# A four-layer graph network on one core: weights loaded in two sets, later waits, an early matrix chunk, and another split of the sorting columns

## The reference

```python
h = relu(layernorm(x)); x = x + L0(h)   # h' = h @ Wn.T; sum over edges of [h'[src], |h'[dst]-h'[src]|] @ We.T; mean; linear
h = relu(layernorm(x)); x = x + L1(h)   # 2 transformer layers: q,k,v; per edge softmax over dst; Wo; FFN 128-512-128 with gelu
h = relu(layernorm(x)); x = x + L2(h)   # relu(D_in^-1/2 A (D_out^-1/2 h) @ W + b)
h = relu(layernorm(x)); x = x + L3(h)   # two GCN convolutions (128-128-64), linear, sigmoid
```

## Time and profile before

| | us |
|---|---|
| median of 3 runs | 7202.54 (7202.37 to 7202.93) |
| the profiled execution's own time | 7193.32 |
| its span, first to last instruction | 7191.1 |
| PE / PEld / DVE / ACT / POOL busy in it | 5421.6 / 3619.8 / 4405.4 / 2900.3 / 3153.2 |
| mean granted TensorE clock | 0.905 of full speed |

### The profile page before, as it was taken

The page is one execution under the profiler, slowest core; times in us unless marked ns, Lnnn a source line. Parts: engine busy times, 40 slices in busy tenths (PEclk is TensorE's granted clock), DMA queues, the critical chain, the costliest instruction groups (busy, mean ns, idle before and its releaser), DMA issues. The chain is left out here.

```text
span 7191.1 us, 122531 instructions
## 1 busy us (share of the span) xinstructions
PE 5421.6 (75%) x28121; PEld 3619.8 (50%) x28122; DVE 4405.4 (61%) x12956; ACT 2900.3 (40%) x5577; POOL 3153.2 (44%) x3144
## 2 busy tenths in 40 slices
PE   7967975777777656666666756666666799999998
PEld 3433433666666545555554545555554444444433
DVE  8969967777777477777777368888885311100000
ACT  2532541677776325555555425555553200000000
POOL 3763772777777007666665007777771000000000
PEclk9989986999999768888888869888887899999999
DMA  0000002555556216666666016666663377777799
GB/s 23 0 3 1 0 0 64 170 171 172 172 172 159 56 39 202 198 199 197 199 198 175 4 43 198 196 196 190 192 194 67 130 289 287 273 286 286 291 417 389
DMA packets 466069, 1168.32 MB, mean 162 GB/s; under 512 B 113598, under 2 KB 176638, under 8 KB 433692
## 3 DMA queue, kind: packets, MB, share of 16 engines
q1 hardware_dynamic: 337228, 892.75, 33.5%
q0 software_dynamic: 126464, 273.15, 15.6%
q10 hardware_dynamic: 2256, 0.89, 0.1%
HBM read 759.86 MB, written 405.32 MB: 162 GB/s over the span
## 5 line engine op out<-in xcount | busy, mean ns | idle before, releaser
L698 POOL DMA_INDIRECT ACC<-tab_kv,STAGE x1664 | 1652.2, 993 | 1440.1 <-DMA STAGE<-IDX 744.0
L1219 ACT ACTIVATE PS<-PS,X 128x512 f32<-128x512 f32 x1456 | 968.4, 665 | 534.4 <-PE PS L904 513.8
L892 PE MATMUL PS<-SCR 128*128 128x137 f32 x3328 | 593.8, 329 | 689.9 <-DVE ACC L1717 681.2
L698 POOL DMA_INDIRECT SCR<-tab_h,STAGE x832 | 829.3, 997 | 345.5 <-issue 275.3
L892 PEld LDWEIGHTS PS<-SCR 128*128 128x128 f32 x3328 | 493.6, 219 | 834.8 <-DVE ACC L1717 791.3
L1717 DVE TENSOR_TENSOR ACC<-ACC,PS 128x137 f32 (+1 forms) x2288 | 746.8, 326 | 248.6 <-PE PS L896 133.6
L1060 PE MATMUL PS<-ACC,Q 128*128 128x512 f32 (+3 forms) x2548 | 842.0, 574 | 59.6 <-DMA ACC<-adj 59.6
L659 POOL DMA_INDIRECT placed<-ACC,X x624 | 649.6, 1041 | 422.4 <-DVE X L1488 219.3
L874 PEld LDWEIGHTS PS<-Q,SCR 128*128 128x128 f32 x4992 | 717.3, 213 | 172.7 <-issue 147.3
L874 PE MATMUL PS<-Q,SCR 128*128 x4992 | 758.2, 300 | 57.5 <-issue 50.1
L765 PE MATMUL PS<-Q 128*128 128x416 f16 x3968 | 721.8, 340 | 59.1 <-DVE Q L1511 59.1
(11 more groups left out here) (297 smaller groups left out, 7437.7 us busy)
## 6 DMA issues: line engine op xcount, KB each, us to landing
ACC<-adj SPq DMA_DIRECT2D x252, 1792.0 KB, 6.7
adj<-X SPq DMA_DIRECT2D x936, 256.0 KB
adj<-ITEM SPq DMA_DIRECT2D x520, 256.0 KB
ACC<-tab_kv,STAGE POOLq DMA_INDIRECT x1664
SCR<-tab_h,STAGE POOLq DMA_INDIRECT x832
tab_kv<-SCR SPq DMA_DIRECT2D x14, 896.0 KB, 4.1
placed<-ACC,X POOLq DMA_INDIRECT x624
ACC<-adj SPq DMA_DIRECT2D x21, 448.0 KB, 4.1
```

Source lines behind the costliest of these rows:

```text
L698: nc.gpsimd.indirect_dma_start(G[:, q, j, 0:w], None, table, bass.IndirectOffsetOnAxis(STAGE[:, u, q * S4 + j:q * S4 + j + 1], 0))\
L892: ins = nc.tensor.matmul(dst, oh, M[:, u % 2, j, :], start=True, stop=True)
L1219: nc.scalar.activation(CLASS_SUM[(k + 1) % 2], CLASS_SUM[k % 2], ACT.Copy, scale=KEEP[:, bass.ds(i, 1)])\
```

## The change

PE's share of the sorting columns becomes 504 (o = 1) and 536 (o = 0), POOL's 280 and 296. `load_l1` is split: `load_d` (14 transfers, what phase d needs) with semaphore `w_d`, `load_e` (8 transfers, what phase e needs) with `w_e`. Layer 1's `load_d` is issued by SP inside att0, behind the first two index loads; its `load_e` after phase e of layer 0. Phase d waits for `w_d`, phase e for `w_e`. DVE's wait for x stands right ahead of the instruction that adds it. SP issues the first matrix chunk in phase e of layer 1, once the last aggregate has been read out of the buffer's place.

```diff
-PROD_COLS = [512, 480]
+PROD_COLS = [536, 504]
...
+        D_MATS, D_ROWS, D_COLUMNS = L1MATS[0:4], [n for n in L1ROWS if n not in ("bo", "b2")], L1COLUMNS[0:2]
+        E_MATS, E_ROWS, E_COLUMNS = L1MATS[4:], ["bo", "b2"], L1COLUMNS[2:]
+        D_LOADS, E_LOADS = len(D_MATS + D_ROWS + D_COLUMNS), len(E_MATS + E_ROWS + E_COLUMNS) + 3
...
-            def load_l1(l):
+            def load_d(l):
+                for n in D_MATS:
+                    sp.dma_start(l1mat[n], a[n][l]).then_inc(w_d, 16)
...
+            def load_e(l):
+                for n in E_MATS:
+                    sp.dma_start(l1mat[n], a[n][l]).then_inc(w_e, 16)
...
-            load_l1(0)
+            load_d(0)
+            load_e(0)
...
                 load(0, 0)
                 load(1, 1)
+                if name == "att0":
+                    load_d(1)
...
+            def tiles(k, g, q):
+                m = chunk(k, g, q)
+                sp.dma_start(TILES3[m % 3][:, :, 0:width(g)], adj[g][:, q * QJ:(q + 1) * QJ, 0:width(g)])\
+                    .then_inc(tiles_in[m % 3], 16)
...
                 if l == 1:
                     sp.dma_start(X[:, :, :], x_rows).then_inc(x_back, 16)
+                    wait(sp, dE[1], "ag", NG)
+                    tiles(0, 0, 0)
                 end_phase(sp, "sp")
                 if l == 0:
-                    load_l1(1)
+                    load_e(1)
...
                         if m >= 3:
                             sp.wait_ge(tiles_used, m - 2)
-                        sp.dma_start(TILES3[m % 3][:, :, 0:width(g)], adj[g][:, q * QJ:(q + 1) * QJ, 0:width(g)])\
-                            .then_inc(tiles_in[m % 3], 16)
+                        if m:
+                            tiles(k, g, q)
...
(DVE; PE and ACT alike)
-                dve.wait_ge(w_l1, 16 * L1LOADS * (l + 1))
+                dve.wait_ge(w_d, 16 * D_LOADS * (l + 1))
...
                 s = dE[l]
-                if l == 1:
-                    dve.wait_ge(x_back, 16)
+                dve.wait_ge(w_e, 16 * E_LOADS * (l + 1))
...
                     if l == 1:
+                        dve.wait_ge(x_back, 16)
                         tail.link(V.tensor_tensor(turn_of(X, g), turn_of(X, g), turn_of(Y, g), ALU.add))
```

More of the change, by code:

```diff
@@ L288, in build @@
         LOADS = len(MATS) + len(BIASES) + 3
-        L1LOADS = len(L1MATS) + len(L1ROWS) + len(L1COLUMNS) + 3
+        D_MATS, D_ROWS, D_COLUMNS = L1MATS[0:4], [n for n in L1ROWS if n not in ("bo", "b2")], L1COLUMNS[0:2]
+        E_MATS, E_ROWS, E_COLUMNS = L1MATS[4:], ["bo", "b2"], L1COLUMNS[2:]
+        D_LOADS, E_LOADS = len(D_MATS + D_ROWS + D_COLUMNS), len(E_MATS + E_ROWS + E_COLUMNS) + 3
         def over_tiles(b, n=TG):
@@ L303, in heads @@
             return ap.rearrange("p t (h d) -> p t h d", h=HEADS)
-        edges_in, x_in, w_in, w_l1, x_pad = sem("edges_in"), sem("x_in"), sem("w_in"), sem("w_l1"), sem("x_pad")
+        edges_in, x_in, w_in, x_pad = sem("edges_in"), sem("x_in"), sem("w_in"), sem("x_pad")
+        w_d, w_e = sem("projection_weights_in"), sem("ffn_weights_in")
         const_ready, const_step = sem("const_ready"), sem("const_step")
@@ L481, in _ @@
         def _(sp):
-            def load_l1(l):
-                for n in L1MATS:
-                    sp.dma_start(l1mat[n], a[n][l]).then_inc(w_l1, 16)
-                for n in L1ROWS:
+            def load_d(l):
+                for n in D_MATS:
+                    sp.dma_start(l1mat[n], a[n][l]).then_inc(w_d, 16)
+                for n in D_ROWS:
                     v = a[n][l, 0] if n == "Wdeg" else a[n][l]
[L487 to L492, removed]
+                    sp.dma_start(row[n], v.partition_broadcast(P)).then_inc(w_d, 16)
+                for n in D_COLUMNS:
+                    sp.dma_start(column[n], a[n][l].rearrange("(k one) -> k one", one=1)).then_inc(w_d, 16)
+            def load_e(l):
+                for n in E_MATS:
+                    sp.dma_start(l1mat[n], a[n][l]).then_inc(w_e, 16)
+                for n in E_ROWS:
+                    sp.dma_start(row[n], a[n][l].partition_broadcast(P)).then_inc(w_e, 16)
+                for n in E_COLUMNS:
+                    sp.dma_start(column[n], a[n][l].rearrange("(k one) -> k one", one=1)).then_inc(w_e, 16)
+                sp.dma_start(WF1[:, :], a["W1"][l]).then_inc(w_e, 16)
+                sp.dma_start(WF2[:, :, :], a["W2"][l].rearrange("(c k) d -> k c d", k=P)).then_inc(w_e, 16)
+                sp.dma_start(B1T[:, :], a["b1t"][l]).then_inc(w_e, 16)
             def load_x(rows, tail, first_tile, signal):
@@ L960, in _ @@
                 s = dD[l]
-                pe.wait_ge(w_l1, 16 * L1LOADS * (l + 1))
+                pe.wait_ge(w_d, 16 * D_LOADS * (l + 1))
                 def normed(g):
@@ L998, in _ @@
                 s = dE[l]
+                pe.wait_ge(w_e, 16 * E_LOADS * (l + 1))
                 def aggregate(g):
@@ L1296, in _ @@
                 norm2 = dict(how=ACT.Identity, scale=column["ln2_g"], bias=column["ln2_b"])
-                act.wait_ge(w_l1, 16 * L1LOADS * (l + 1))
+                act.wait_ge(w_d, 16 * D_LOADS * (l + 1))
                 def self_exp(g):
@@ L1321, in _ @@
                 s = dE[l]
+                act.wait_ge(w_e, 16 * E_LOADS * (l + 1))
                 def gelu(g, *cs):
```

## The result

The changed kernel takes 7117.61 us (median of 5 runs, 7117.32 to 7134.75); the kernel before, timed beside it, 7202.52 us (5 runs, 7198.92 to 7202.93). That is 84.9 us less, where the prediction's sum was 92.5. The kernel is faster, by about 1.1%, clear of noise. The profiled execution took 7118.68 us with a span of 7116.9, 74.2 us under the span of before; before's profiled execution lay 9.2 us under its median, this one 1.1 us over, which is most of the distance between 74.2 and 84.9.

What follows compares the result with a forecast made beforehand. It took POOL's transfers to bound both sort passes, with three waits between phases also on the path; 55.9 + 17.4 + 13.85 + 6.8 - 1.5 = 92.5 us off 7202.5 gave 7110.0 us, range 7104 to 7116.

Steps and rivals of the forecast that it cites:

- Sort: Both sort passes: moving 24 columns each from POOL to PE gains 28.5 and 27.4 us, 55.9 us in all.
- rival (b): Sort passes: POOL slows further when DVE is busy throughout, giving 7150 us, or 7130 with half the effect; chance 0.05.
- Weights: Head of phase d of layer 1: loading its weights in att0 cuts DVE's wait from 17.62 to 0.23, gaining 17.4 us.
- x: Head of phase e of layer 1: waiting for x only at its first use gains 13.85 us.
- First chunk: Start of the matrix stream: issuing the first chunk early lets PE start after the barrier, gaining 6.8 us.
- rival (e): Start of the matrix stream: the early chunk gains nothing since PE then waits for the second; 7117 us, chance 0.04.
- The 14 loads at att0's head: Start of att0: the moved loads delay the first gathers, costing 1.5 us, with bounds of 0 and 6.7.
- Rival (a): Start of att0: loads hold it up by SP's issue time, 6.7 us or perhaps twice that; 7115 to 7122, chance 0.10.
- Rival (c): Edge passes: their clock drifts, shifting the time by 10 us in both to 7100 or 7120; chance 0.12.
- the prediction's own sign: Attention passes: the prediction is wrong if the two together change by more than 10 us.
- The step from the profile to the median: Whole kernel: the median stays 9.2 us above the profiled execution, which goes from 7193.3 to 7100.8 us.

Runs made afterwards that it cites:

- e11: The changed kernel with DVE's wait for x back at the head of phase e of layer 1; 8737.44 us, ratio 0.9953, on a slower chip.
- e10: The changed kernel without the early load of the first matrix chunk, issued behind the end of phase e as before; 8725.94 us, ratio 0.994, on a slower chip.
- e13: The changed kernel again, unaltered, on a chip where the kernel before takes 7190.31 us; 7111.98 us, ratio 0.9881.
- e12: The changed kernel with 4 matrix loads plus 8 added ones at att0's head, row and column loads moved to phase e; ratio 0.9948 on a slower chip.
- e3: e1's kernel plus one transfer of 0.79 MB in 6 KB pieces at att0's head; ratio 0.9915 on a slower chip.
- e2: The changed kernel with 12 more matrix loads of 64 KB behind the 14 at att0's head; ratio 0.9905 on a slower chip.
- e5: The changed kernel with the 14 loads moved from att0 to the head of phase e of layer 0; 7095.36 us, ratio 0.9867.
- e9: The changed kernel again, unaltered, on a slower chip where the kernel before takes 8776 us; 8719.89 us, ratio 0.9932.
- e1: The changed kernel with the 14 loads moved from att0 to the head of phase e of layer 0; ratio 0.9922 on a slower chip.
- e4: The kernel before with only the column split changed to 536/504; ratio 0.9968 on a slower chip where the kernel before takes 8860 us.
- e14: The kernel before with only the column split changed to 536/504, on a chip where the kernel before takes 7190.31 us; 7137.11 us, ratio 0.9923.

## Why the prediction was right where it was, and where it failed

- **Sort, 55.9 us.** Right. 29.1 and 26.7 us (55.8) in the first profile, 54.7 with the split alone. PE's side sets the end, as worked out; the first pass ended at 500.1 (forecast 500.7), the second at 1026.0 (1054.4 less the first pass's 28.5 is 1025.9). POOL's pace stayed too: (494.39 - 110.06) / 279 = 1.378 us a transfer, so rival (b), POOL slower when DVE is busy throughout, did not happen.
- **Weights, 17.4 us.** Right: 17.62 became 0.21. The second set's new wait shows nowhere.
- **x, 13.85 us.** Right: 14.00 became 0.21, and e11 brings 13.8 back.
- **First chunk, 6.8 us.** Right: 6.95 in the first profile (16.48 less 9.53), 6.7 by e10. The second chunk costs nothing; rival (e) falls.
- **The 14 loads at att0's head, -1.5 us.** This is the step that failed. They cost 7.8 us in the first profile (9.65 to 17.49), 6.8 in e13, more than the upper bound of 6.7. The prediction took 1.5 from a transfer time of 2.5 us "at the 317 GB/s of the seam where only chunks move". That rate is the one of another kind of transfer; these loads moved 91 GB/s, gathers included. The seam of before in which the very same loads ran among the 22, at 85 GB/s, was the nearer row; at that rate 0.79 MB take 9.3 us. SP's issue time, which the prediction did weigh, was not what mattered either: twelve loads issued at the same pace held nothing up in e12. The gathers, on POOL's own queue, were held, and only by the row loads. The Trainium skill ("DMA: Bandwidth & Descriptors", "SWDGE vs HWDGE vs iDMA"), which the prediction cites, says that the DMA engines serve both kinds of queue in turn. The traces agree that loads on the one queue can hold up gathers on the other (7.8 us), but the 2.5 us that the prediction worked out by that rule is a third of it for the rows, and for as many bytes of matrices (e12) or in one transfer (e3) no delay shows.
- **Rival (a), 0.10.** It is what happened, in part. Its result (7115 to 7122) holds the measured 7117.6, but its reason (the issue time on SP, perhaps a stalled ring of stores) is not the one the runs show: e12 has 12 such commands and the same bytes on SP and no late group, e3 the same bytes, and e2 has 26 commands and no later group than 14 give. No stalled ring of stores shows in the changed kernel (ACT waits for no store between 2640 and 2800 us). That this rival's time came out is luck: the price was the right size for another reason.
- **Rival (c), the edge passes drift, and the prediction's own sign.** It called itself wrong "if the two attention passes together change by more than 10 us". They did: att0 from its first index load to phase e went from 1262.7 to 1273.9 us, att1 from 1150.3 to 1156.6, 17.5 us in all. Of that 7.8 are the row loads; the other 9.7 are of the size by which these stretches vary (e5: 1263.2 and 1151.7), and whether a part of them belongs to the change is open.
- **The step from the profile to the median.** The sum was worked out on the profiled execution and forecast 7100.8 us for the next one, which took 7118.7, 17.9 more: 6.3 by the row loads, the rest is no more than the stretches of e9 and e13 above vary by. The median came out nearer, 7.6 us from the forecast, because the profiled execution of before lay 9.2 us under its median and the new one did not. The prediction left that distance as it was without a reason; that it made the miss smaller is luck.

With 7.8 in the place of 1.5 the sum is 86.2 us and the time 7116.3; measured were 7117.6, 84.9 us less than before, and, on another chip, 78.3 us less. The three versions with the rows at att0's head that were timed on chips where the kernel before takes about 7200 us have ratios 0.9891, 0.9878, 0.9881, the three without them 0.9867, 0.9870, 0.9870: on average 0.0014 apart, 10 us, whose single intervals of 0.0012 to 0.002 to either side would not show it. On the two slower chips the times even lie the other way (e2 with the rows 0.9905, e1 and e3 without 0.9922 and 0.9915; e9 with them 0.9932, e12 without 0.9948), also inside the intervals. So it is the traces, stretch by stretch, that show the cause, and not the times. The ratios of both sets of runs, 71 to 87 and 74 to 96 us, hold the 86.2, so the times don't show that anything else is missing.

## What to carry to other kernels

Price a moved load by its own kind: look in the trace for the same load where it ran before, its time from issue to landing and the GB/s of that stretch, and not for the best rate of any transfer. A load moved off one seam can cost where it lands if another seam's first transfers start there; put it where the engines have work ahead. Two terms that should meet, like POOL's and PE's side of the sort, are settled by one run on either side of the split.

## What the runs showed of the hardware

- **Spread rows are slow and hold up others.** Eight loads that spread a 512-byte row over 128 partitions land one behind the other (3.6 to 10.1 us), with the DMA engines busy a third of the time, and with them DVE's first group, which waits for indirect gathers on another queue, comes at 16.2 to 17.5 us; with twelve loads of the same 64 KB from distinct rows it comes at 9.7, without any load at 9.05 to 9.65. Why one source row read 128 times costs more was not tried further.
- **Chips on which the sort's loop stands still while POOL's transfers run.** On the two slower chips the changed kernel's first pass ends at 853.6 us (e9) instead of 501.3 (e13). The windows of e9, first while POOL's indirect transfers run, then behind them, show why:

```profile
200.00:300.00 100.00, 10.20 (x32) 4.27 (x32) 5.77 (x20) 3.36 (x8) 73.81 (x78) 0.53 0.02 1
...
560.00:660.00 100.00, 96.09 (x527) 48.79 (x526) 91.79 (x328) 54.67 (x131) 0.00 (x0) 1.00 0.00 0
```

In 100 us PE does 32 matmuls beside 78 transfers and 527 without them; in the changed kernel's first profile it does 526 beside 72 in the same window. POOL itself is not slowed. DVE's waits there name no releaser of this program:

```profile
DVE Q L1534 <- remote: 313.2, 10, 42.0
```

Seven of these ten, and one more whose wait the view calls "issue", are 40.6 to 42.0 us long, one every 45 us, and the last ends at 498.8, after the last transfer (476.1). The sort then gains by fewer transfers (24 x 1.31 = 31 us a pass) and pays for more columns (18.3), an estimate of 26 us for both passes from e9's pace and the turns of the earlier trace rows; it fits the 22.5 us of the split alone (e4) against 53.2 on the other chip (e14), but no profile of the kernel before was taken on such a chip. The edge passes are longer there as well: att1 takes some 1495 us in e9 where it takes 1161 in e13, with 285 us of DVE's waits put down to no releaser of this program. What holds the engines up was not found.
